# Issuing both halves of a tile's scores back to back on TensorE in the six-layer stacks

## The reference

```python
# shift_tokens moves the second half of the features by one token
qkv = shift_tokens(x) @ Wqkv                     # 16 heads of 64
q = l2norm(q) * qs;  k = l2norm(k) * ksc         # then rotary embedding of both
sim = einsum('bhwie,bhwje->bhwij', bq, bk2) * 8  # windows of 32 queries, 64 keys
attn = softmax(where(mask, -max, sim))
x = (attn @ bv2) @ Wo + x
x = (a * gelu(gate)) @ W2 + b2 + x               # a, gate = LN(shift_tokens(x)) @ W1 + b1
```

## Time and profile before

| | |
|---|---|
| time, median of 3 runs | 3809.59 us (3805.08 to 3809.89) |
| span of the profiled execution | 3803.9 us |
| PE busy | 3594.4 us, 94% |
| DVE busy | 3264.6 us, 86% |
| POOL busy | 2752.8 us, 72% |
| ACT busy | 2374.7 us, 62% |
| granted TensorE clock in both stacks | 1.00, which is 2.4 GHz |

### The profile page before, as it was taken

The page is one execution under the profiler, slowest core; times in us unless marked ns, Lnnn a source line. Parts: engine busy times, 40 slices in busy tenths (PEclk is TensorE's granted clock), DMA queues, the critical chain, the costliest instruction groups (busy, mean ns, idle before and its releaser), DMA issues. The chain is left out here.

```text
span 3803.9 us, 157044 instructions
## 1 busy us (share of the span) xinstructions
PE 3594.4 (94%) x61680; PEld 2336.5 (61%) x61680; DVE 3264.6 (86%) x11515; ACT 2374.7 (62%) x4331; POOL 2752.8 (72%) x2632
## 2 busy tenths in 40 slices
PE   6799999999999999997699689999999999999998
PEld 4466666666666666662466456666666666666665
DVE  6898888888888889865799798889898888889885
ACT  2567667666766767663422257667676766767665
POOL 1788888878888888852144288888887888888883
PEclk9899999999999999998799699999999999999999
DMA  1232323323322332220000132233233232332222
GB/s 46 77 85 71 81 73 78 87 67 74 85 73 69 85 75 66 66 65 16 0 1 6 29 81 72 74 87 78 71 80 76 71 81 74 83 78 68 66 69 57
DMA packets 170286, 250.95 MB, mean 66 GB/s; under 512 B 36544, under 2 KB 67264, under 8 KB 169408
## 3 DMA queue, kind: packets, MB, share of 16 engines
q1 hardware_dynamic: 169536, 240.72, 25.4%
HBM read 38.21 MB, written 1.05 MB: 10 GB/s over the span
## 5 line engine op out<-in xcount | busy, mean ns | idle before, releaser
L592 PE MATMUL stack_work<-stack_w_qkv,stack_xs 128*128 128x512 f32 x2304 | 1148.0, 604 | 34.4 <-ACT stack_sq L883 17.8
L1244 POOL TENSOR_TENSOR stack_roped<-stack_rot_c,stack_rot_s 128x512 f32<-128x512 f32 x768 | 984.6, 1304 | 148.5 <-DVE stack_rot_s L1052 148.2
L1254 POOL TENSOR_TENSOR stack_roped<-stack_roped,stack_rnorm 128x512 f32<-128x512 f32 x768 | 794.6, 1045 | 188.7 <-DVE stack_rnorm L1084 188.7
L883 ACT ACTIVATE stack_sq<-stack_work 128x512 f32<-128x512 f32 x768 | 443.3, 594 | 485.6 <-DVE stack_rot_s L1052 485.1
L1050 DVE TENSOR_TENSOR stack_rot_c<-stack_work,rot_tables 128x512 f32<-128x512 f32 x768 | 526.8, 686 | 130.4 <-PE stack_work L592 112.9
L592 PEld LDWEIGHTS stack_work<-stack_w_qkv,stack_xs 128*128 128x128 f32 x2304 | 400.5, 191 | 384.4 <-issue 323.9
L1270 POOL TENSOR_TENSOR stack_s_m<-stack_s_m,stack_inv 128x512 f32<-128x512 f32 x384 | 400.8, 1044 | 276.4 <-DVE stack_inv L1113 276.1
L1052 DVE TENSOR_TENSOR stack_rot_s<-stack_work,rot_tables 128x512 f32<-128x512 f32 x768 | 521.6, 679 | 0.0
L1061 DVE TENSOR_REDUCE stack_ssq<-stack_sq 128x8 f32<-128x512 f32 x768 | 496.7, 667 | 6.0 <-issue 4.4
L641 PEld LDWEIGHTS stack_bank_o<-stack_p_t,stack_v_w 64*64 64x64 f32 x24576 | 394.5, 135 | 171.9 <-issue 147.4
L600 PE MATMUL stack_work<-ident,stack_roped 128*128 128x128 f32 x3072 | 452.2, 280 | 8.3 <-issue 5.8
(11 more groups left out here) (257 smaller groups left out, 5269.0 us busy)
## 6 DMA issues: line engine op xcount, KB each, us to landing
stack_v_w<-stack_v_nat SPq DMA_DIRECT2D x1152, 128.0 KB
stack_v_w<-stack_v_nat SPq DMA_DIRECT2D x768, 64.0 KB
stack_w_qkv<-table_ffn_qkv SPq DMA_DIRECT2D x192, 96.0 KB, 2.3
stack_w_o<-table_ffn_wo SPq DMA_DIRECT2D x12, 512.0 KB, 4.2
stack_w<-table_ffn_w SPq DMA_DIRECT2D x12, 384.0 KB, 3.3
stack_w<-table_ffn_w SPq DMA_DIRECT2D x12, 192.0 KB, 3.1
x_outer<-L_attn_a_X SPq DMA_DIRECT2D x4, 256.0 KB, 6.9
ret_xpos<-table_xpos SPq DMA_DIRECT2D x1, 1024.0 KB, 6.2
```

The source lines that it names most:

```text
L592: pe.matmul(bank[:, :], xs[:, T, :], w_qkv[:, g.half, col:col + 512], start=True, stop=True).then_inc(done["proj_" + c], 1)
L883: act.activation(sq[:, i % 2, :], work[(BANK["p_" + c][T] + g.row) % 4][:, :], ACT.Square).then_inc(done["squared_" + c], 1)
L1244: pool.tensor_tensor(roped[:, i, T % 2, :], rot_c[:, i % 2, :], rot_s[:, i % 2, :], ALU.add).then_inc(done["roped_" + c], 1)
L1254: pool.tensor_tensor(r, r, rnorm[:, T % 2, i, :].unsqueeze(2).broadcast_to([P, 8, HD]), ALU.mult).then_inc(done["united_" + c], 1)
```

## The change

In each of the four kinds of slot, the wait for `masked1` and `scores` of part 0 are taken from behind `project q0` and put directly ahead of `scores` of part 1. Nothing else moves. The blocks in between (turn_probs 0, project_out, weigh 0, turn k1, project k1, the feed-forward block and project v0) now follow `project q0` directly. Tiles, operands, other engines and the DMA queue are as before.

```diff
                     wait(pe, "kept_k0", N - 4)
                     project(*at(2), "q0", work[(3 + row) % 4])
-                    wait(pe, "masked1", N - 5)
-                    scores(*at(4), 0)
                     wait(pe, "pt_set1", N - 6)
                     turn_probs(*at(6), 0, work[(0 + row) % 4])
...
                     wait(pe, "mid_set", N - 7)
                     project(*at(4), "v0", work[(1 + row) % 4])
+                    wait(pe, "masked1", N - 5)
+                    scores(*at(4), 0)
                     scores(*at(4), 1)
```

## The result

The changed kernel takes 3835.07 us (median of 4 runs, 3832.23 to 3839.59) against 3807.34 us for the kernel before in the same series: a ratio of 1.0075, 95% interval 1.0061 to 1.0090. It is slower by 28 us. The forecast was 3829 us and slower, from a range of 3800 to 3852.

A forecast was written before the change was run, and what follows sets the result against it. TensorE's order was taken to set the time. Slot sums of +0.44, 0, -0.29 and +0.31 us gave +0.46 per cycle, 19.3 us over 42, and with 5.7 us above the span 3829 us, range 3800 to 3852.

The forecast's parts named there:

- What is saved on TensorE: Per slot on TensorE alone: 0.94 us from removing the first burst, less X of 0.65, saves 0.29 us.
- X: Time of 64 more matmuls in the open burst ahead of part 1: taken as 0.65 us, range 0.57 to 0.75.
- The waits: Three PE waits per cycle: ScalarE's squares some 0.6 us, VectorE's `hid` some 0.5, ScalarE's `hid` 0.75 instead of 0.44.
- T = 3: Slot from `down` to `project q1`: `project k1` waits for q0's square, 0.62 us becomes wait; sum +0.44 us.
- T = 2: Slot where `turn_probs` waits for `hid1`: only 0.34 of 0.94 us can be pulled forward; sum +0.31 us.
- T = 0: Slot up to `up gate 1`: the 0.29 us only lengthen the GELU wait, from 0.46 to 0.75; sum 0.
- T = 1: Slot from `up gate 1` to the next `project q1`: inputs fit by 0.20 us, no wait; sum -0.29 us.
- The first rival, no binding waits,: VectorE and ScalarE chains close up, three of four slots each win 0.29 us: -36.5 us, 3773 us, chance 0.13.
- The second and third rival: Second: long burst at first part's pace, X 0.54, 3815 us, chance 0.22; third: nothing saved, X 0.79, 3847 us, chance 0.15.
- The size: Over both stacks: 42 cycles at +0.46 us make 19.3 us; nothing taken for the run-ups.
- The base: Whole kernel: 5.7 us, by which the median lies above the profiled span, added to about 3823 us.

The follow-up runs named there:

- The kernel with the halves late but apart: The changed kernel, but in all four slots `project v0` and its wait stand between the two parts of the scores: ratio 1.0191.
- the single-slot kernels: The change in one kind of slot alone, kernel before otherwise: for T = 0, 1, 2, 3 the ratios are 0.9999, 0.9979, 1.0036, 1.0041.
- the swap: The changed kernel with `project k1` and the gate product exchanged in T = 3: ratio 1.0029; with T = 2 left as before also, 0.9987.
- the earlier `hid1`: Kernel before with the change in T = 1 and T = 2, and VectorE's product raising `hid1` ahead of the norm's first step: ratio 0.9954.
- the earlier table: Kernel before with the change in T = 0 alone, and ScalarE's GELU table loaded ahead of the square of k1: ratio 0.9915.
- the one with doubled scores: The kernel before with the first half of the scores issued twice in a row at its old place, in all four slots: ratio 1.0378.
- the one tried alone: Kernel before with only VectorE's product that raises `hid1` moved ahead of the norm's first step: ratio 0.9994.

## Why the prediction was right, step by step

- **What is saved on TensorE.** X was 0.65 us, as taken, and 0.94 - 0.65 = 0.29 us were won where nothing else bound. The kernel with the halves late but apart shows that it is the joining that saves it.
- **The waits.** All three stand where they were placed. The prediction put their sizes in the profile at 0.6, 0.5 and 0.75 us, where the view of waits shows 0.32, 0.38 and 0.62; the first two were delays by starts, not idle times. Counted by starts, as the forecast's sum was, T = 3 loses 0.60 us of the 0.62 put down to it: `weigh` starts 36.79 - 34.76 - 1.88 = 0.15 late for the copy ahead of it, `project k1` 38.80 - 37.86 - 0.49 = 0.45 (the 1.88 and 0.49 are the same steps in the trace before, below). `turn_probs` in T = 2 starts 82.58 - 80.31 - 1.72 = 0.55 late, as forecast (0.54). The wait for GELU was to grow to 0.75 in idle time and reads 0.61: the other 0.12 us of T = 0 are lost earlier, ahead of `weigh`, a wait that the forecast didn't name. The segment's sum, 0, is the same. T = 1 fitted.

The timeline of PE in slot T = 3 of the kernel before, between rows:

```profile
1029.26 1.14 PE L641 MATMUL stack_bank_o<-stack_p_t,stack_v_w 64*64 64x32 f32 x64
1030.33 0.66 PE L600 MATMUL stack_work<-ident,stack_roped 128*128 128x128 f32 x4
```

- **The first rival, no binding waits,** is answered by the single-slot kernels: T = 0, 2 and 3 gain nothing or lose, each by its own wait, and each comes out below before once that wait is taken away: T = 3 by 0.13 us with the swap, T = 2 by 0.28 with the earlier `hid1`, T = 0 with the earlier table by 0.85, most of which is the old wait.
- **The second and third rival** put X at 0.54 or 0.79. The trace shows 0.65.
- **The size.** 42 cycles at 0.46 us gave 19.3 us; the medians differ by 27.7 and the two profiled spans by 26.5. The direction and the typical cycle were right, the total was 30% short. One term that was too small is the cycle's mean. The sum of the 38 regular cycles rose by 21.3 us, 0.56 a cycle, where 17.5 were forecast for them: 0.45 to 0.50 as a typical cycle, and the rest in stalls of long bursts, which had no term. From first to last matmul start, 42 of 192 bursts after and 14 of 384 before were over 0.02 us longer than the typical one, together some 5 us against 1. The rest of the difference between the spans, 5 us, lies in the two cycles with a loop branch (+5.6), the run-up and drain of the stacks (+4) and the mixer's stretch (-5). The change doesn't touch the mixer, whose stretch with the second run-up ran from 620 to 628 us over all kernels here, so I take that part for scatter. A cycle with a loop branch ran from 69.6 to 75.4 us, but not all of that is scatter: TensorE's hole behind the branch lasted 4.5 to 5.1 us in the five kernels with the pair in T = 3, the slot just ahead of the branch, and 3.4 to 4.1 us in the nine others. So about 1 us a branch belongs to the change, and the forecast had no term for it.
- **The base.** I added 5.7 us to the span, as the median of the first runs lay above it. In the changed kernel the profiled execution's time is only 1.8 us above its span, 3832.23 against 3830.4; the rest of the 5.7 was the spread between executions. That it brought the forecast nearer to the measured time is luck.

Open: what makes long bursts stall. Holes of over 0.2 us inside a burst occur 79 times in the 14 traces, and 71 of the 74 in bursts of 128 come behind the 103rd matmul or later. In the kernel after there are four: behind the 121st at 600.96 and 1139.88 us and behind the 120th at 2610.04 and 3148.24 us, so each stack shows the same place of the program in both passes of its loop. The trace's DMA records tie the holes to the supply of instructions: ahead of the end of every one of the 79, by 1.10 to 1.63 us, a packet of 16 KB of the instruction queue landed, while only 11% of the other matmuls inside bursts have one at a distance of 1.0 to 1.7 us. With 20% more instructions for TensorE that queue carried 595 packets against 499, and the holes became common. This is a tie in time; no run changes the supply alone, so the cause is not shown.

## What to carry to other kernels

Moving a block later on the engine that sets the pace pulls what stood behind it forward, and its own cost comes later all the same. So ask slot by slot for the slack of each input that is pulled forward (its use minus its readiness in the trace before): where it is less than the pull, the gain turns into a wait and the sum into a loss. Then look for the input's delay as well as for the order: one swap on TensorE and two steps on other engines, of which the one tried alone was worth nothing, turned a loss of 0.75% into a gain of 1.4%. Not all of that gain is the pair's: of the 1.49 us won per cycle, 0.73 are by the sum above the old wait for GELU, which stood there without the change.

## What was not expected of the hardware

- A burst of 128 small matmuls (256 instructions with the weight loads) runs at 10 ns a matmul and now and then stops late in its course, for up to 0.86 us in the kernel after and 1.66 us in the one with doubled scores. Bursts of 64 did so five times in the kernel with the halves apart, for up to 0.81 us, and in no other kernel here. The Trainium skill (TensorE: Matmul & The Clock Gate, Wait — 56ns, not 53.3ns?) has matmuls start no closer than about 25 ns, however small they are; for these matmuls on parts of the array the trace disagrees, since the second 64 take 0.65 us.
- A projection behind a wait takes 0.97 us to the next start instead of 0.86, in the kernel before and after alike, and the idle time shown for a wait is 0.16 us shorter than the delay by starts (0.46 against 0.62 for GELU before). By starts, a wait shown as 0.46 us so cost 0.62 + 0.11 = 0.73.
